# Attention and expert kernel: other engine orders and PSUM banks, and first-batch key features made with that batch's own maximum

## What is computed

```
x   = x + tanh(g_x) * performer(layernorm(x), ctx, ctx)
        h_k    = -0.5 * sum(k*k);  k_stab = max(h_k)        # one maximum over all batches, heads and tokens
        k'     = exp(h_k + k@F - k_stab) + 1e-4             # key features, F is 16 x 64
        q'     = exp(q@F) + 1e-4                            # query features
        out_t  = q'_t . sum_{s<=t} k'_s v_s / (q'_t . sum_{s<=t} k'_s)
u   = layernorm(x);  h = rmsnorm(u) * gamma1
x2  = u + softmax(q k / 4) v @ Wo + bo                      # q from Wq, k and v from Wup(Wdown(h)), per token over heads
out = x + tanh(g_f) * (x2 + sum_e gate_e * (rmsnorm(x2) * gamma2) @ We[e])
```

## Time and profile before

| | us |
|---|---|
| median of three runs | 1119.69 |
| the profiled execution, its own time | 1119.66 |
| its span, first to last instruction | 1117.9 |
| TensorE (PE) busy | 1034.7 |
| VectorE (DVE) busy | 938.5 |
| ScalarE (ACT) busy | 757.0 |
| GpSimd (POOL) busy | 756.8 |

### The profile page before, as it was taken

How to read it: one execution, slowest core, us unless ns; L and a number is a source line. 1 busy time by engine, 2 the same in 40 slices (tenths; PEclk the granted TensorE clock), 3 DMA queues, 4 the chain that set the end, 5 groups by cost and what they waited for, 6 DMA issues and landing times.

```text
span 1117.9 us, 31579 instructions
## 1 busy us (share of the span) xinstructions
PE 1034.7 (93%) x12867; PEld 841.2 (75%) x12867; DVE 938.5 (84%) x2173; ACT 757.0 (68%) x1563; POOL 756.8 (68%) x1111
## 2 busy tenths in 40 slices
PE   0576899999999999999999999999999999999988
PEld 0355677778888888778888787888778888888776
DVE  7578678888888988888888888888888988888886
ACT  6666767667776776777677667776776677767531
POOL 3467776677767767777777667776767777777431
PEclk9988899999999999999999999999999999999999
DMA  9410000100001001010010101000000000000000
GB/s 307 142 29 11 21 30 1 30 30 30 30 30 29 11 21 30 30 30 30 30 31 2 29 30 30 30 30 30 24 8 31 29 31 30 30 30 12 11 11 19
DMA packets 38911, 38.63 MB, mean 35 GB/s; under 512 B 3440, under 2 KB 38512, under 8 KB 38768
## 3 DMA queue, kind: packets, MB, share of 16 engines
q1 hardware_dynamic: 38384, 36.59, 10.5%
q0 software_dynamic: 384, 0.04, 0.0%
HBM read 28.23 MB, written 8.39 MB: 33 GB/s over the span
## 4 chain that ended last, share of the span: by engine, by line
PE 52%; DVE 24%; DMA 7%; ACT 7%; POOL 6%; issue 2%; SPq 1%; POOLq 0%; DVEq 0%; ACTq 0%
PE ps L1857 10%; PE ps L1858 7%; PE ps L1859 7%; DVE z L1142 6%; PE ps L1888 6%; PE ps L1903 5%; PE ps L1872 4%; DMA c_in<-in_ctx 4%; DMA x_in<-in_x 3%; PE ps L1937 3%; PE ps L1896 3%; POOL x L424 2%; POOL z L417 2%; DVE k_t L1426 2%; PE ps L1851 2%
## 5 line engine op out<-in xcount | busy, mean ns | idle before, releaser
L1142 DVE SCALAR_TENSOR_TENSOR z<-ps,gate,z 128x256 f32<-128x256 f32 x512 | 234.5, 470 | 17.4 <-PE ps L1859 8.9
L1857 PE MATMUL ps<-we_hi,h_hi 128*128 128x512 f32 (+2 forms) x640 | 238.8, 373 | 5.8 <-DVE s_sub L1296 1.7
L1858 PE MATMUL ps<-we_lo,h_hi 128*128 128x512 f32 (+2 forms) x640 | 223.7, 350 | 0.0
L1859 PE MATMUL ps<-we_hi,h_lo 128*128 128x512 f32 (+2 forms) x640 | 223.7, 349 | 0.0
L1857 PEld LDWEIGHTS ps<-we_hi,h_hi 128*128 128x128 f32 x640 | 120.2, 188 | 44.3 <-issue 18.5
L1888 PE MATMUL ps<-qf,kf 64*128 64x256 f32 x1024 | 137.4, 397 | 11.7 <-POOL qf L408 9.4
L1859 PEld LDWEIGHTS ps<-we_hi,h_lo 128*128 128x128 f32 x640 | 120.2, 188 | 17.2
L1858 PEld LDWEIGHTS ps<-we_lo,h_hi 128*128 128x128 f32 x640 | 120.5, 188 | 11.6
L1888 PEld LDWEIGHTS ps<-qf,kf 64*128 64x128 f32 x1024 | 95.1, 191 | 36.9 <-issue 19.1
L1903 PE MATMUL ps<-att,v 128*32 128x256 f32 (+1 forms) x2048 | 112.4, 339 | 1.2 <-DVE att L1218 0.9
L475 POOL TENSOR_SCALAR v_bd<-v_t,sel_blk 128x512 f32<-128x512 f32 x128 | 88.3, 710 | 13.2 <-DVE v_t L1249 13.2
(11 more groups left out here) (218 smaller groups left out, 3077.9 us busy)
## 6 DMA issues: line engine op xcount, KB each, us to landing
x_in<-in_x SPq DMA_DIRECT2D x32, 256.0 KB, 3.3
c_in<-in_ctx SPq DMA_DIRECT2D x32, 256.0 KB, 3.7
out<-z SPq DMA_DIRECT2D x32, 256.0 KB, 2.2
c_chunk<-in_ctx SPq DMA_DIRECT2D x14, 512.0 KB, 8.9
stage<-in_L_ffn_We SPq DMA_DIRECT2D x2, 1024.0 KB, 9.6
c_chunk<-in_ctx SPq DMA_DIRECT2D x2, 256.0 KB, 8.5
stage_u<-in_L_ffn_Wup SPq DMA_DIRECT2D x2, 128.0 KB, 5.7
stage_b<-in_L_ffn_bup SPq DMA_DIRECT2D x1, 256.0 KB, 6.1
```

Source lines behind the costliest of these rows:

```text
L1142: return dve.scalar_tensor_tensor(out=z[b % 2][:, t, :], in0=ps[:, bank, offset:offset + D], scalar=gate[:, t, ex:ex + 1], in1=z[b % 2][:, ...
L1857: pe.matmul(out, a_hi(c), b_hi(c), start=(c == 0), stop=False)
L1858: pe.matmul(out, a_hi(c), b_lo(c), start=False, stop=False)
L1859: last = pe.matmul(out, a_lo(c), b_hi(c), start=False, stop=(c == C - 1))
```

## The change

- Every engine's order is another, both the list ahead of the slots and the slot itself. TensorE now has its first six turns and its last four batches written out; slots run for n = 6 to 30.
- The bank table is another.
- `kf` no longer shares memory with the chunk buffers; `z` and `x1` do instead.
- The key features of batch 0 are made with the maximum of batch 0 alone (`first`). When the maximum of all is known, alpha = exp(first - stab) is formed, and the pk steps of batch 0, which added 1e-4, now compute kf * alpha + 1e-4 in the same instruction.
- `load_x_(1)` is issued before the chunks instead of after them, the expert weights `We` before the other weights instead of after them.
- More steps signal: the list of signals grows from 36 to 57 entries, and more steps wait, since the new orders don't imply the old ones' guarantees.

```diff
-        with ExitStack() as early:
-            c_chunk = [sb_early(f"c_chunk{n}", [P, CH * T, D]) for n in range(CHUNK_BUFFERS)]
-        kf = sb("kf", [P, PAIRS, L])
+        kf = sb("kf", [P, PAIRS, L])
+        with ExitStack() as early:
+            c_chunk = [sb_early(f"c_chunk{n}", [P, CH * T, D]) for n in range(CHUNK_BUFFERS)]
...
+            def first_least_():
+                dve.wait_ge(*at("key_sums", 0))
+                dve.tensor_reduce(first_col[:, :], hk[:, 0:T, :], AX.XY, ALU.min).then_inc(*up("first_least"))
+            def first_most_():
+                dve.wait_ge(*at("first_turned"))
+                dve.tensor_reduce(first_one[:, :], ps[0:1, BANK["first"], 0:P], AX.X, ALU.min).then_inc(*up("first_most"))
+            def first_():
+                dve.wait_ge(*at("first_all"))
+                dve.tensor_scalar(first[:, :], ps[:, BANK["first"], P:P + 1], -0.5, None, ALU.mult).then_inc(*up("first"))
+            def less_first_():
+                dve.wait_ge(*at("first"))
+                dve.tensor_scalar(hk_first[:, :, :], hk[:, 0:T, :], -0.5, first[:, 0:1], ALU.mult, ALU.subtract).then_inc(*up("less_first"))
-            def less0_():
...
+            def alpha_():
+                act.wait_ge(*at("kept"))
+                act.activation(alpha[:, :], stab[:, :], ACT.Exp, scale=-1.0, bias=first[:, 0:1]).then_inc(*up("alpha"))
...
             def pk0_(b):
+                if b:
+                    last = pool.tensor_scalar(tokens_of(kf, 0), tokens_of(kf, 0), KERNEL_EPS, 1.0, ALU.add, ALU.mult)
+                else:
+                    last = pool.tensor_scalar(tokens_of(kf, 0), tokens_of(kf, 0), alpha[:, 0:1], KERNEL_EPS, ALU.mult, ALU.add)
...
             # TensorE, ahead of the slots
-            most_turned_()
-            stab_all_()
-            fkp_(0)
-            fk_(0)
+            first_turned_()
+            first_all_()
+            fkp_(0)
+            fk_(0)
+            fq_(0)
+            most_turned_()
+            stab_all_()
+            X00_(0)
...
             # TensorE, the slot
-                mm1g_(n - 7) av2_(n - 4) pv_(n - 6) av3_(n - 4) mm10_(n - 7) fq_(n - 3) kv1_(n - 5) mm00_(n - 7)
-                o_tr_(n - 6) kv0_(n - 5) mm11_(n - 7) o_(n - 6) nt_t_(n - 4) mm12_(n - 7) mm01_(n - 7)
-                X01_(n - 3) X00_(n - 3) Y0_(n - 3) mm02_(n - 7) mm03_(n - 7) mm13_(n - 7) h2_t1_(n - 6) h2_t0_(n - 6)
-                hn_t_(n - 4) av0_(n - 3) s_(n - 5) av1_(n - 3) X11_(n - 3) Y1_(n - 3) X10_(n - 3)
-                qq_(n - 4) dn_(n - 4) mm0g_(n - 6) fkp_(n - 2) fk_(n - 2)
+                h2_t1_(n - 3) h2_t0_(n - 3) mm13_(n - 4) dn_(n - 1) fq_(n + 1) mm1g_(n - 3) mm0g_(n - 3)
+                o_tr_(n - 2) mm12_(n - 3) kv0_(n - 1) kv1_(n - 1) o_(n - 2) mm10_(n - 3) mm11_(n - 3)
+                X00_(n + 1) X01_(n + 1) Y0_(n + 1) Y1_(n + 1) X11_(n + 1) X10_(n + 1) av0_(n + 1) s_(n - 1) av1_(n + 1)
+                mm00_(n - 3) mm01_(n - 3) hn_t_(n) mm02_(n - 3) fkp_(n + 2) av2_(n + 1) pv_(n - 1) av3_(n + 1)
+                fk_(n + 2) mm03_(n - 3) nt_t_(n + 1) qq_(n)
```

More of the change, by code:

```diff
@@ new lines, in build @@
+            signal("pe0", "fk fq X00 Y1"),
+            signal("pe1", "X01 X11 av3 nt_t"),
+            signal("pe2", "Y0 X10"),
+            signal("pe3", "av0 av1"),
+            signal("pe4", "hn_t qq s"),
+            signal("pe5", "dn kv0"),
+            signal("pe6", "kv1 pv"),
+            signal("pe7", "o_tr o h2_t0"),
+            signal("pe8", "h2_t1 mm1g mm10 mm11"),
+            signal("pe9", "mm0g mm12"),
+            signal("pe10", "mm00 mm01 mm03"),
+            signal("pe11", "mm02 mm13"),
@@ L640, in nt0_, with h_t_ @@
+            @per_batch
+            def h_t_(b):
+                if b >= 0:
+                    act.wait_ge(*at("h_tr", b))
+                act.activation(h_t[:, :], h_raw[:, :], ACT.Copy).then_inc(*up("h_t", b))
             @per_batch
@@ new lines, in d_lo_, with h_tr_ @@
+            @per_batch
+            def d_lo_(b):
+                dve.wait_ge(*at("d_hi", b))
+                dve.scalar_tensor_tensor(out=down[R:P, :], in0=ps[R:P, BANK["dn"], 0:L], scalar=bdn_col[R:P, 0:1],
+                                         in1=down[R:P, :].bitcast(F32), op0=ALU.add, op1=ALU.subtract).then_inc(*up("d_lo", b))
+            @per_batch
+            def h_tr_(b):
+                if b >= 0:
+                    dve.wait_ge(*at("h_lo", b))
+                if b >= 1:
+                    dve.wait_ge(*at("h_t", b - 1))
+                dve.transpose(blocks(h_raw), h2e[:, :, :, :].rearrange("p t a k -> p (t a) k")).then_inc(*up("h_tr", b))
@@ new lines, in q_t_, with ga_ @@
+            @per_batch
+            def q_t_(b):
+                dve.wait_ge(*at("bqq", b))
+                dve.transpose(q_t[:, :, :].rearrange("p n h -> p h n"), qkv[:, :, 0:D].rearrange("p t (h d) -> p h t d", d=HD)).then_inc(*up("q_t", b))
+            @per_batch
+            def ga_(b):
+                dve.wait_ge(*at("mm0g", b))
+                if b >= 0:
+                    dve.wait_ge(*at("mm1g", b))
+                for t in range(T):
+                    last = dve.tensor_tensor(ga[:, t, :], ps[:, BANK[f"mm{t}g"], D:D + E], b_g[:, :], ALU.add)
+                last.then_inc(*up("ga", b))
@@ new lines, in o_ @@
+            @per_batch
+            def o_(b):
+                if not b:
+                    pe.wait_ge(*at("bqq", b + 1))
+                if b >= 4 and b + 3 < NB:
+                    pe.wait_ge(*at("eq3", b + 3))
+                pe.wait_ge(*at("ot_lo", b))
+                for t in range(T):
+                    last = three_passes(ps[:, BANK["o"], t * D:(t + 1) * D], tok(ot_hi, t), tok(ot_lo, t), cols(wo_hi, 0, D), cols(wo_lo, 0, D))
+                last.then_inc(*up("o", b))
+            @per_batch
```

2952 lines of the change are left out of this document (1814 added, 1138 removed).

## The result

The changed kernel takes 1069.43 us (median; 1068.09 to 1069.6). The kernel before, run beside it, takes 1120.68 us. The ratio is 0.954, with a 95% interval of 0.9512 to 0.9568: 51 us less. The forecast was 1088.2 and its range began at 1070.0, so the direction was right and the size was 19 us off, just outside the range. The probes (p1, p2, f1, f2, f3) were run twice each, the others four times or more; one of the four executions of e2_tile2 took 3984.75 us and is counted in its median of 1087.21, which is 1086.82 without it.

The account below looks back on a forecast made before the run. Engine-to-engine chains were taken to bound the fill and TensorE the turns. Fill 140 + 27 turns of 31.7 (855.9) + end 90.5 + 1.8 outside the span = 1088.2 us, range 1070 to 1112.

Parts of the forecast that it names:

- "1.7": Start: the maximum over all batches is kept 1.7 us later than before, at 36.6 us; bounds 0 and 4.
- rival D: Head start doesn't reach the rest: maximum late by 4, or POOL held by weight remainders; 1098.6 to about 1112 us; chance 0.08.
- 140 between 133 and 150: Fill: X of batch 4 starts at 140 us, between DVE's work at 87% (133) and nothing gained (150.4).
- 3.5 us "for chained latencies": Fill: 3.5 us added to the 136.5 from stepping through the new orders, for latencies that this leaves out.
- The walk: Fill: stepping through the new orders put X of batches 1 to 4 at 58.5, 80, 105 and 136.5 us.
- the sum of what goes: Turns: 0.85 us less TensorE time a turn, from fewer shape changes and two waits; 32.2 to 31.35.
- terms for mm00 and for bqq: Turns: removed waits, 0.3 us a turn at mm00 and 0.25 for the bqq addition ahead of the key products.
- the 0.3 added for tight waits: Turns: 0.3 us a turn added for tight places (av0, s, fkp) and DVE's load, giving 31.7.
- rival E: Slower: a loop across turns on ACT, late k_bd delaying later steps; 33.2 us a turn, 1131 us; chance 0.07.
- half of the 11 us: End: at best half of TensorE's 11 us idle time there goes, at worst 2 longer; 2 taken, giving 90.5.
- rival C: Everything hidden as laid out: X of batch 4 at 135, 31.3 a turn, end 88; 1070 us; chance 0.12.
- B: Rival: turns keep their length, each removed stall coming back as a tight wait; 1102 us; chance 0.20.

Follow-up runs that it names:

- p1: The changed kernel with one more POOL instruction of 128x512 ahead of mask m01 in each of 25 slots; 1081.46 us.
- p2: The changed kernel with one more DVE instruction of 128x512 ahead of y00 in each of 25 slots; 1072.84 us.
- f1: The changed kernel with one more POOL instruction ahead of the first feature step of each of batches 1 to 4; 1070.60 us.
- f2: The changed kernel with one more DVE instruction at four places ahead of steps on which batches 1 to 4 depend; 1071.23 us.
- f3: The changed kernel with one more ACT instruction at four places in the fill (ahead of h_t(1), k_hi(2), k_hi(3), xn(3)); 1070.20 us.
- e2_tile2: The changed kernel with the third pass of fq inside the gate products mm1g, two more tile shape changes in each of 25 turns; 1087.21 us.
- e7: The kernel before with only batch 0's head start (own maximum, rescaling), old orders and banks from batch 1 on; 1116.07 us, ratio to before 0.9992.
- e4: The changed kernel with one expert-weight remainder on DVE made later, after the second products of batch 0 are copied; 1069.09 us.
- e3: The changed kernel with norm products fk directly behind feature products fkp in 25 slots, 8 tile shape changes a turn instead of 9; 1067.85 us.
- e12: The changed kernel with fk next to fkp, y01 ahead of g_bn on DVE, and POOL's four v_bd instructions split over three places; 1061.11 us.
- e5: The changed kernel with POOL's four v_bd instructions directly behind masks m01 and m00 instead of ahead of them, in 25 slots; 1101.37 us.
- e8: The changed kernel with POOL's four v_bd instructions behind q_r instead of ahead of the masks, in 25 slots; 1079.79 us.
- e10: The kernel before with batch 0's head start and the expert weights' load issued right behind the chunks; 1115.49 us, ratio to before 0.9969.

## Why the prediction was off, point by point

**What bounds the kernel.** Right: fill bound by chains, turns by TensorE. The turns of after are packed to 843.3 of 844.1 us.

**The start.** The chain was right (alpha, then four rescaling rows, X at 39.4 for 39.7), its terms were not. The "1.7" for the maximum coming later is 0.1 against before (34.94 for 34.85), the four rows take 3.9 us instead of 2.7: 0.85 by the collision that rival D named, in one of them, and the rest by rows of 0.69 instead of 0.62. "The rescaling itself costs nothing" was off by these 0.07 us a row. The gain at X of batch 0 is 5.3 us, inside the bounds of 3 and 7.

**The fill, 6.5 us of the miss.** The failed step is the choice of 140 between 133 and 150, and in it the 3.5 us "for chained latencies". The walk was 3 us too short up to X of batch 1 (61.5 for 58.5), where TensorE still waits 4.1 us for POOL, and 6 us too long from there to X of batch 4 (72 for 78); the latencies were then added where the walk was already long. Two things were left out altogether. The first is which work lies in this part: twelve expert products, 2.8 us, now come after X of batch 31, so that much of the miss here is no gain of the kernel. The second is TensorE's own speed. From X of batch 0 to X of batch 4 TensorE is busy for 88.8 us before and for 79.4 after. The granted clock of the two middle stretches was 0.87 and 0.84 before and is 0.92 and 1.00 after. So of the 16.6 us that this part became shorter, 7.2 are idle time gone (21.9 for 14.7), 2.8 are the twelve products, and 6.6 are the other products taking less time. The clock can give about that: a stretch with granted clock c in which TensorE is always busy loses (1 - c) of its length, which over the stretches is 10.3 us before and 3.4 after, an estimate of at most 6.9 from these rows. (The clock column shows 1.00 for the first stretch of before, though its X group, 3.79 us for sixteen products, is at the lower level; the same holds for the X group at 39.44 after.) A pair of rows shows the two levels: the X group at 61.54 has 2.08 us for eight products, which is 1.2 GHz, the one at 133.47 has 2.00 for sixteen, 2.4 GHz. In the stretch that ends at 61.54 TensorE is busy for 14.7 of 22.1 us, in the one that ends at 133.47 for 25.3 of 27.1. My bounds took TensorE's share as given. e7 goes with this: head start, old lists, the same clocks of 0.87 and 0.84 as before, and 113.5 us for this part. But no run changes the idle time alone, and e4 had less of it than after (13.8 us) at a lower clock, so how the one leads to the other is open. Nor does any run tell which of the new orders shortened the fill.

**The turns, 11.7 us of the miss.** The failed steps are two sizes, and a rounding of 31.65 to 31.7, which is 1.4 us over 27 turns. The first size is the sum of what goes, 0.85 in the forecast. A shape change costs 0.20 us (e2, e3), so two fewer are 0.40, not 0.3. The terms for mm00 and for bqq came as forecast. At mm00 0.29 us a turn are gone (0.31 for 0.12 ahead of it, 0.34 for 0.23 behind). At the key products it was 0.51 where a change alone takes 0.21, and is 0.38 where it takes 0.33, so 0.25 are gone; no wait for bqq is left in the rows. Not in the sum were 0.04 at the transposes h2_t (0.15 for 0.11), and waits for ACT, 2.3 us in three, which lie in the first three of the 27 turns, 0.09 on the average of 27. This makes 1.07. The second size is the 0.3 added for tight waits. The wait that I named first (av0 behind m00) exists, but is worth 0.09 in after. e12, without any wait in its list and with one change less, has 30.88 a turn; with the change, 0.20, that is TensorE's own time, 31.08, and 0.14 is left for all waits of after (31.22). So the base was 31.1, not 31.35, and the margin 0.14, not 0.3. 1.07 gone less 0.14 new is 0.93, and 0.95 was measured. The extra signals and waits, taken at nothing, show nothing on TensorE: in both kernels a product of 128x256 follows at 0.12 and one of 128x512 at 0.23. Orders and bank table were changed together in every run, so what each gives is not separated. What I got right is what the margin was for: p1 shows that 0.7 us more on POOL ahead of the masks is 0.54 us a turn at once, e5 and e8 that the same v_bd at other places costs 1.33 and 0.45, and rival E's mechanism, a late step on ACT behind hn, is what e5 turned on.

**The end.** 90.0 for 90.5, by luck. TensorE's idle time fell from 11.3 to 6.1 us, all of the "half of the 11 us" that the text gave at best, and the twelve products from the fill added 2.7 us of busy time (83.9 for 81.2), of which the forecast had nothing. That the twelve come later is seen from the counts; no run tested the end.

**The rivals and the range.** The time is rival C's to 0.6 us (1070), not by its terms (135, 31.3 and 88 against 133.5, 31.27 and 90.0), but by its idea: everything hidden as laid out. C had a chance of 0.12 because I gave each tight place its own doubt and added the doubts up. The lower bounds that the text itself named (133 for the fill, 31.2 a turn, and for the end 87, half of its 11 us gone) would have summed to 133 + 842.4 + 87 + 1.8 = 1064.2. The range stopped at C's rounded terms instead, and the result fell 0.6 us below it. B is refuted by the turns. D's collision is real (1.54 us for 0.69 in the start), but taking it away gave nothing that can be measured (e4).

## What to carry to other kernels

When a list of instructions is laid out by hand and closes with the bounding engine packed, the time to forecast is that engine's own sum, and the range has to reach the sum of its lower bounds; a margin for tight places belongs in the upper half only. Price a head start together with what is queued behind it: alone it ended at two loads in turn (e7, e10), and only with lists that put the next batch ahead of the late weights did it arrive. And in a pipeline that fills, read the bounding engine's busy time and clock as well as its gaps: here the busy time gave back 6.6 us beside the 7.2 of the gaps. Before the parts of two kernels are compared, count the instructions in each.
